# Two token blocks of a pair share one transposition each for h1c and h2c

## The reference

```python
x = x + einsum('bct,bcd->bdt', x, w0[adapter])
x = x + einsum('bsi,io->bso', x, W1) + (x @ A1[adapter]) @ B1[adapter]
x = x + einsum('bsi,oi->bso', x, W2) + 0.5 * (x @ A2[labeler]) @ B2.T
logits = x @ Wr.T + 5.0 * one_hot(language, 8)
gates  = sum over top 2 of one_hot(expert) * softmax(top 2 logits)
x = x + x @ W3.T + 2.0 * einsum('bter,bte,eor->bto', x @ A3, gates, B3)
```

## Time and profile before

| | |
|---|---|
| Median of 3 runs | 521.34 us (521.17 to 521.99) |
| The profiled execution, device time | 521.43 us |
| Its span, first to last instruction | 519.6 us |
| Granted clock of TensorE | 1.00 |
| TensorE, matmul, busy | 515.1 us, 99% |
| DVE busy | 334.2 us, 64% |
| ACT busy | 201.9 us, 39% |
| POOL busy | 170.2 us, 33% |
| Chain that ended last, share on TensorE | 98% |
| Matmuls of `part`, t_hi x em_hi (the costliest line) | 168, 57.3 us, 403 ns each |

### The profile page before, as it was taken

How to read it: one execution, slowest core, us unless ns; L and a number is a source line. 1 busy time by engine, 2 the same in 40 slices (tenths; PEclk the granted TensorE clock), 3 DMA queues, 4 the chain that set the end, 5 groups by cost and what they waited for, 6 DMA issues and landing times.

```text
span 519.6 us, 8870 instructions
## 1 busy us (share of the span) xinstructions
PE 515.1 (99%) x2720; PEld 450.4 (87%) x2720; DVE 334.2 (64%) x655; ACT 201.9 (39%) x351; POOL 170.2 (33%) x250
## 2 busy tenths in 40 slices
PE   8999999999999999999999999999999999999997
PEld 8999999988988888888887888888888888888886
DVE  4798886799533333399876864756647557476464
ACT  5744653345222222267344233323333333233322
POOL 2550000002102020219546544354254434552400
PEclk9999999999999999999999999999999999999999
DMA  7911210214430202040703303313233042222312
GB/s 263 374 65 40 60 40 1 82 40 125 158 112 0 82 0 82 0 166 4 242 2 118 121 23 119 100 47 108 83 117 121 34 117 86 69 87 81 120 32 81
DMA packets 29631, 46.80 MB, mean 90 GB/s; under 512 B 12052, under 2 KB 17940, under 8 KB 29476
## 3 DMA queue, kind: packets, MB, share of 16 engines
q1 hardware_dynamic: 29268, 45.72, 27.3%
q0 software_dynamic: 192, 0.59, 0.3%
q10 hardware_dynamic: 144, 0.13, 0.1%
HBM read 33.39 MB, written 13.04 MB: 89 GB/s over the span
## 4 chain that ended last, share of the span: by engine, by line
PE 98%; DVE 1%; ACT 0%; issue 0%; POOL 0%; POOLq 0%; DVEq 0%; ACTq 0%
PE bank L1893 26%; PE bank L1827 15%; PE bank L1759 11%; PE bank L1882 8%; PE bank L1801 6%; PE bank L1730 5%; PE bank L1813 5%; PE bank L1973 4%; PE bank L1941 4%; PE bank L1949 4%; PE bank L1714 3%; PE bank L1944 1%; PE bank L1943 1%; PE bank L1903 1%; PE bank L1721 1%; PE bank L1930 0%
## 5 line engine op out<-in xcount | busy, mean ns | idle before, releaser
L1893 PE MATMUL bank<-t_hi,em_hi 128*128 128x512 f32 x168 | 57.3, 403 | 0.0
L1183 DVE TENSOR_TENSOR w1t_lo<-raw,w1t_hi 128x1024 fp32r<-128x1024 f32 x18 | 24.1, 1339 | 23.6 <-ACT w1t_hi L909 17.1
L684 POOL TENSOR_TENSOR tmp<-raw 128x512 f32<-128x512 f32 x4 | 7.2, 1793 | 97.2 <-DVE raw L1369 97.2
L1893 PEld LDWEIGHTS bank<-t_hi,em_hi 128*128 128x128 f32 x168 | 31.1, 188 | 7.2 <-DVE em_hi L1183 0.4
L1827 PE MATMUL bank<-te,em_hi 128*128 128x512 f32 x144 | 34.9, 395 | 0.0
L1827 PEld LDWEIGHTS bank<-te,em_hi 128*128 128x128 f32 x144 | 27.0, 188 | 6.6
L670 POOL CAST em_hi<-tba 128x256 fp32r x32 | 13.4, 447 | 58.3 <-PE bank L1882 54.6
L1183 DVE TENSOR_TENSOR em_hi<-tmp,em_hi 128x512 fp32r<-128x512 f32 x22 | 15.1, 688 | 21.7 <-ACT em_hi L1016 12.6
L674 POOL TENSOR_TENSOR em_lo<-tba,em_hi 128x256 fp32r<-128x256 f32 x32 | 27.1, 868 | 2.4 <-POOL em_hi L670 1.2
L1759 PE MATMUL bank<-em_hi,w2s_hi 128*128 128x384 f32 x80 | 27.0, 337 | 0.0
L1759 PE MATMUL bank<-em_lo,w2s_hi 128*128 128x384 f32 x80 | 26.9, 337 | 0.0
(11 more groups left out here) (309 smaller groups left out, 1615.2 us busy)
## 6 DMA issues: line engine op xcount, KB each, us to landing
raw<-in_x_dram SPq DMA_DIRECT2D x16, 512.0 KB, 4.2
b1s<-b1scr SPq DMA_DIRECT2D x32, 217.5 KB, 2.8
raw<-in_b1w_dram SPq DMA_DIRECT2D x10, 512.0 KB, 3.6
out_dram<-ef SPq DMA_DIRECT2D x16, 256.0 KB, 2.1
out_dram<-ost SPq DMA_DIRECT2D x15, 256.0 KB, 2.5
graw<-in_w3a3wr_dram SPq DMA_DIRECT2D x4, 768.0 KB, 11.0
...
```

Source lines behind the costliest of these rows:

```text
L1183: V.tensor_tensor(dst, src, f32(hi), ALU.subtract).then_inc(signal, 1)
L1893: ins = nc.tensor.matmul(to[:, :], left[a][:, k0 + k, :], m_right(right, z, k), start=(name in OPENS and n == 0), stop=(n == 3 * KH - 1), ...
```

## The change

Pair 0, 1 and 7 keep their order. For pairs 2 to 6 (`JOINT`), each engine gets a list of its own:

- h1c of both blocks stand side by side in one tile of 128 columns (without the second copy of the high piece), and TensorE transposes them at once, after three matmuls of p7. The same for h2c, with one transposition after 10 matmuls of p3. Both results lie in bank 6.
- The pieces that are needed more than once are copied by ACT when it empties the bank: four copies instead of one per block for h1T (two for each block), six for h2T (three for each block).
- `h1_into` of both blocks stand after 9 matmuls of p7, `h2_into` of both after 7 of p4. So `route` and `gates` of b0, once beside p6 and p2, and those of b1 come after that. `gated_across` of b0 stands within the `narrow` after p4, that of b1 between tile 1 and tile 2.
- ACT's split of the next pair's XA (`left_hi`) stands ahead of the h2 copies.
- The rows of b1s are interleaved between the two batch rows of a block; in `b1scr` the order of thirds is hi, hi, lo. The place of the bias table goes to h1c; POOL copies the bias elsewhere before pair 0.

The end of the pair's list on DVE, before. gh is the gates' product of b1 (bank 7); em_hi from bank 2 is the split of bank C for tile 2, xb_lo from bank 1 that of bank B for tile 3; the copies to ef and ost3 are tiles 1 and 3; em_lo from bank 5 is `xn_lo`.

The diff, cut to its core:

```diff
-    bias = small("bias", [P, NB, E])
+    bias0 = at("bias0", [P, NB, E], F32, q[0])
+    h1c = small("h1c", [P, 2 * PER * 2 * R1], F32R)
+    assert 2 * PER * 2 * R1 == NB * E
...
+    H1_THREE = h1c[:, 0:2 * SEG1].rearrange("p (t r h) -> p t r h", t=3, h=PER)
+    H1_BOTH = h1c[:, :].rearrange("p (s z r h) -> p s z r h", s=2, z=2, h=PER)
+    H2_BOTH = h2c[:, :, :].rearrange("p (s z) r -> p s z r", s=2)
 
...
+        JOINT = range(2, NP - 1)
+        TH_LAST, HTS_LAST = -2 * len(JOINT), 6 * len(JOINT)
+        SMALL = {n: i + 1 for i, n in enumerate((("mixed", 0), ("mixed", 1), ("h1", 0), ("h1", 1), ("h2", 0), ("h2", 1)))}
+        H1_COPIES, H2_COPIES = 2, 3
+        COPIES = 2 * (H1_COPIES + H2_COPIES)
...
-                    for third, half in enumerate((0, 1, 0)):
+                    for third, half in enumerate((0, 0, 1)):
...
-                    rows = slice(h * SEG1, (h + 1) * SEG1)
+                    rows = slice(h, PER * SEG1, PER)
...
+            pool.wait_ge(s_cst, E + 4)
+            for s in range(2):
+                nc.gpsimd.tensor_copy(BIAS[:, s, :].rearrange("p (b e) -> p b e", e=E), bias0[:, s:NB:2, :]).then_inc(s_bias, 1)
...
+            def h1_both(p):
+                act.wait_ge(s_th, th_joint(p) + 1)
+                for s in range(2):
+                    own = slice(4 * R1 * s, 4 * R1 * (s + 1))
+                    own_hi = slice(4 * R1 * s, 4 * R1 * s + 2 * R1)
+                    nc.scalar.activation(h1T[s][0:4 * R1, :], bank[RT][own, Z1], ACT.Copy).then_inc(s_hts, 1)
+                    nc.scalar.activation(h1T[s][4 * R1:6 * R1, :], bank[RT][own_hi, Z1], ACT.Copy).then_inc(s_hts, 1)
+            def h2_both(p):
+                act.wait_ge(s_th, th_joint(p) + 2)
+                for s in range(2):
+                    own = slice(2 * R2 * s, 2 * R2 * (s + 1))
+                    own_hi = slice(2 * R2 * s, 2 * R2 * s + R2)
+                    nc.scalar.activation(h2T[s][0:R2, :], bank[RT][own_hi, Z2], ACT.Copy).then_inc(s_hts, 1)
+                    nc.scalar.activation(h2T[s][R2:2 * R2, :], bank[RT][own_hi, Z2], ACT.Copy).then_inc(s_hts, 1)
+                    nc.scalar.activation(h2T[s][2 * R2:4 * R2, :], bank[RT][own, Z2], ACT.Copy).then_inc(s_hts, 1)
 
...
+            def joint_pair_hi(p):
+                b0, b1 = 2 * p, 2 * p + 1
+                made = PRODUCTS * p - PRODUCTS
...
+                xn_hi(b1, YB)
+                act.wait_ge(s_sum, 4 * p - 1)
+                operand_hi(XB[0][:, 0:KH, :], tmp[:, :, :])
+                h1_both(p)
+                act.wait_ge(s_wide, made + PRODUCT["p7"])
+                left_hi(p + 1)
+                h2_both(p)
+                xm_hi(0, bank[BA])
+                exp_of(b0)
+                act.wait_ge(s_wide, made + PRODUCT["p3"])
+                xm_hi(1, bank[BD_])
+                ght_hi(b0, 0)
+                exp_of(b1)
+                xn_hi(b0 + 2, YB + 1, 6 * p + SMALL["mixed", 1])
+                act.wait_ge(s_add, 3 * p)
+                act.wait_ge(s_mix, 4 * p + 1)
+                xm_hi(0, bank[BC])
+                ost_even(p, 0)
+                act.wait_ge(s_wide, made + PRODUCT["p4"])
+                act.wait_ge(s_mix, 4 * p + 2)
+                xm_hi(1, bank[BB])
+                ght_hi(b1, 1)
+                ost_even(p, 2)
...
+            def joint_pair_lo(p, steps):
+                b0, b1 = 2 * p, 2 * p + 1
+                ops = OPS * p - OPS
+                operand_lo(CS[1], tmp[:, :, :], CS[0], ops + 2)
+                first_joint(0, 6 * p + SMALL["mixed", 0], steps)
+                operand_lo(DS[1], tmp[:, :, :], DS[0], ops + 3)
+                operand_lo(XB[1][:, :, :], raw[1][:, :, :], XB[0][:, :, :], ops + 4)
+                sum_p1(p)
+                operand_lo(CS[1], raw[1][:, 0:KH, :], CS[0], ops + 5)
+                sum_p5(p)
+                xn_lo(b1, YB)
+                operand_lo(XB[1][:, 0:KH, :], tmp[:, :, :], XB[0][:, 0:KH, :], ops + 6)
+                first_joint(1, 6 * p + SMALL["mixed", 1], steps)
+                second_joint(0, 6 * p + SMALL["h1", 0], steps)
+                sum_p7(p)
+                second_joint(1, 6 * p + SMALL["h1", 1], steps)
+                left_lo(p + 1)
+                route(p, 0, steps, 6 * p + SMALL["h2", 0])
+                xm_lo(0, bank[BA], 4 * p + 1)
+                gates(b0, 0, steps)
+                route(p, 1, steps, 6 * p + SMALL["h2", 1])
+                xm_lo(1, bank[BD_], 4 * p + 2)
+                ght_lo(b0, 0)
+                xn_lo(b0 + 2, YB + 1)
+                gates(b1, 1, steps, b0 + 1)
+                xm_lo(0, bank[BC], 4 * p + 3)
+                xm_lo(1, bank[BB], 4 * p + 4)
+                ght_lo(b1, 1)
+                ost_odd(p, 1)
+                ost_odd(p, 3)
...
-            def narrow(b, left, to):
-
-                pe.wait_ge(s_sel, 4 * b + 4)
-                if isinstance(b, int) and b == 0:
-                    pe.wait_ge(s_s0l, 1)
-                above(pe, s_xnl, b)
-                for k in range(K):
+            def narrow(b, left, to, ks=range(K)):
+                if ks.start == 0:
+                    pe.wait_ge(s_sel, 4 * b + 4)
+                    if isinstance(b, int) and b == 0:
+                        pe.wait_ge(s_s0l, 1)
+                    above(pe, s_xnl, b)
+                for k in ks:
                     for a, z in TERMS:
                         ins = nc.tensor.matmul(bank[to][:, 0:SC], left(a, k), S[z][:, k, :], start=(k == 0 and (a, z) == TERMS[0]),
                                                stop=(k == K - 1 and (a, z) == TERMS[-1]), skip_group_check=True)
-                ins.then_inc(s_nar, 1)
+                if ks.stop == K:
+                    ins.then_inc(s_nar, 1)
 
...
+            def h1_both_across(p):
+                pe.wait_ge(s_h1c, 4 * p + 4)
+                nc.tensor.matmul(bank[RT][:, Z1], f32(h1c[:, :]), ident[:, :], is_transpose=True, start=False, stop=True,
+                                 skip_group_check=True).then_inc(s_th, 1)
+            def h2_both_across(p):
+                pe.wait_ge(s_h2c, 4 * p + 4)
+                nc.tensor.matmul(bank[RT][:, Z2], f32(h2c[:, :, :]).rearrange("p m r -> p (m r)"), ident[:, :], is_transpose=True,
+                                 start=False, stop=True, skip_group_check=True).then_inc(s_th, 1)
...
+            def joint_pair_products(p):
+                b0, b1 = 2 * p, 2 * p + 1
+                ops, sums = OPS * p - OPS, 3 * p - 3
+                h1_there = hts_joint(p) + 2 * H1_COPIES
+                h2_there = hts_joint(p) + COPIES
+                part("p1", 0, 5)
+                mixed(b0, 0)
+                part("p1", 5, 12)
+                pe.wait_ge(s_opl, ops + 2)
+                part("p5", 0, 12)
+                pe.wait_ge(s_opl, ops + 3)
+                part("p6", 0, 12)
+                pe.wait_ge(s_opl, ops + 4)
+                narrow(b1, second_block, YB)
+                pe.wait_ge(s_cp, 2 * p - 1)
+                part("p2", 0, 7)
+                mixed(b1, 1)
+                part("p2", 7, 12)
+                pe.wait_ge(s_add, sums + 2)
+                pe.wait_ge(s_opl, ops + 5)
+                part("p7", 0, 3)
+                h1_both_across(p)
+                part("p7", 3, 9)
+                h1_into_from(h1_there, 0, p)
+                h1_into_from(h1_there, 1, p)
+                part("p7", 9, 12)
+                pe.wait_ge(s_opl, ops + 6)
+                part("p3", 0, 10)
+                h2_both_across(p)
+                part("p3", 10, 12)
+                pe.wait_ge(s_add, sums + 3)
+                part("p4", 0, 7)
+                h2_into_from(h2_there, 0)
+                h2_into_from(h2_there, 1)
+                part("p4", 7, 12)
+                pe.wait_ge(s_opl, ops + 7)
+                narrow(b0 + 2, first_block, YB + 1, range(0, 6))
+                gated_across(b0, 0)
+                narrow(b0 + 2, first_block, YB + 1, range(6, K))
+                tile(p, 0, False, False)
+                tile(p, 1, False, False)
+                gated_across(b1, 1)
+                tile(p, 2, False, False)
+                tile(p, 3, False, False)
```

More of the change, by code:

```diff
@@ L56, in cond_resid_kernel @@
     ROWS = LORA + K
+    NP_ = NB // 2
     F3C = 3 * P
@@ L1520, in first_low_rank, with first_joint, second_joint @@
                     ts, at_ = slice(h * T, (h + 1) * T), C3 + PER * R2 + h * R1
-                    lo(h1c[ts, h * SEG1 + 2 * R1:(h + 1) * SEG1], nar[ts, at_:at_ + R1], h1c[ts, h * SEG1:h * SEG1 + R1], s_h1c)
+                    lo(H1_THREE[ts, 1, :, h], nar[ts, at_:at_ + R1], H1_THREE[ts, 0, :, h], s_h1c)
+            def first_joint(s, there, steps):
+                nar = bank[RT + s]
+                dve.wait_ge(s_small, there)
+                for h in range(PER):
+                    ts, at_ = slice(h * T, (h + 1) * T), C3 + PER * R2 + h * R1
+                    steps.then(V.tensor_copy(H1_BOTH[ts, s, 0, :, h], nar[ts, at_:at_ + R1]))
+                steps.hold()
```

(41 more changed lines are left out.)

56 lines of the change are left out of this document (42 added, 14 removed).

## The result

| | before | after |
|---|---|---|
| Median | 521.39 us (521.17 to 521.99, 5 runs) | 534.08 us (533.72 to 534.69, 5 runs) |
| Ratio after / before, 95% interval | | 1.0242 [1.023, 1.0253] |
| Span of the profiled execution | 519.6 us | 532.2 us |

A forecast was written before the change was run, and what follows sets the result against it. TensorE's chain of slots was taken as the bound; stalls of 0.13 + 0.06 + 0.61 + 0.3 less 0.22 made +0.9 us a joint pair (+0.6 the first), together +4.2, so 525.5 us, range 522.6 to 528.1.

The forecast's parts named there:

- The rest, at nothing: Bias copies, interleaved b1s rows (as many DMAs as before), the split of `narrow` and narrower casts on DVE: no cost.
- Tile 1's copy and SP: Tile 1's copy on DVE ends later, XB follows 11.37 us behind through SP's stores: TensorE stalls about 0.3 us a pair.
- the first has no late XB yet: The first joint pair is spared the XB stall, so it loses 0.6 us instead of 0.9.
- The left operand holds up the h2 copies: Rival, chance 0.08: x lands late, ACT's split delays the six h2 copies, +0.5 us a pair on top, 528.1 us.
- Copies at eviction: ACT's four h1T and six h2T copies fit with 0.13 and 0.4 us spare: no cost.
- Gates of block 0: From the first `h2_into` to gh's end takes 3.48 us against TensorE's 3.39: stall 0.13 us a pair.
- Gates of block 1: On DVE beside POOL's subtractions they take 2.61 us: stalls of 0.06 at gh's transposition and 0.61 at tile 2.
- The rival in which they run clear of it: Rival, chance 0.20: block 1's gates take 1.60 us instead of 2.61, away from POOL; +1.3 in all, 522.6 us.
- Ten transpositions fewer: Two fewer on TensorE in each of five pairs, 0.11 us each: 0.22 a pair, 1.1 us saved.
- Pair 7: Keeps the old order; its spare 0.5 us swallows the 0.3 of late XB; its b1s may come 0.1 late.
- Sums: TensorE slot totals: 3.39 us to block 0's gh, 4.55 from its end to block 1's, 17.8 to XB's use.
- What would show it: Right: TensorE's longest wait at tile 2 (some 0.5), then XB, pairs 0.9 longer; wrong: ACT-copy waits larger than DVE's.

The follow-up runs named there:

- e1: The changed kernel with each batch row's b1s rows in neighbouring partitions again instead of every second one (only the time is read): 527.89 us, ratio 1.0108.
- e9: The changed kernel with one edit: GpSimd's `take` for the second block waits until gh of block 1 is written: 533.62 us, ratio 1.0237.
- e12: The changed kernel with SyncE's loads reordered (pairs 1 to 6), `take` behind the gates, two TensorE steps later, `ght_lo` ahead of bank D's split: 521.07 us, ratio 0.9992.

## Why the prediction was wrong, step by step

- **The rest, at nothing**: the failed step. "b1s rows are interleaved but as many DMAs as before" counted the DMAs and not what each costs SyncE. At 0.51 instead of 0.33 us they add 1.4 us a pair to a chain that the prediction itself had given 0.5 to spare. e1 prices that line at some 6.2 us of 12.7; without it the kernel takes 527.89, inside the forecast range.
- **Tile 1's copy and SP**: right in kind, wrong in size, +1.04 for +0.3. From the copy's end (384.05 + 0.68) to that of XB's low half (395.44 + 1.23) it took 11.94 instead of 11.37, with four of the dear issues in it. The longer gates moved tile 2 and the copy alike: the copy ended 1.34 behind tile 2's first matmul, 1.27 had been forecast. That "the first has no late XB yet" failed too: SyncE's list of pair 1 holds the same issues, TensorE waited 0.6 for XB in the first joint pair, and that pair lost 2.3 instead of 0.6.
- **The left operand holds up the h2 copies**, given 0.08: it came true, with +0.38 a pair. Its condition was a late landing of x; the landing was at least as quick as assumed (3.14), but the issue was not where the earlier trace rows had it. The rival took the issue as fixed behind XB's end, 7.27 us as before; it was 8.11 (396.67 to 404.78). It should have been asked of this rival what else moves the issue, and what follows from tile 1's copy depending on x: a ring, in which a delay is paid in every round instead of once.
- **Copies at eviction**, at nothing: +0.21 at `h1_into`. The copies follow each other at 0.29, not 0.22 (the 0.22 of the earlier trace rows is between instructions of another kind); the prediction had named 0.3 as the point from which 0.1 is lost, and took the lower value.
- **Gates of block 0**: right in kind; 0.29 for 0.13.
- **Gates of block 1**: 2.9 for 2.61 in three of the five pairs, 2.5 in the first and the last; +0.88 for +0.67 in the pair of the table. Right that they stand beside GpSimd's subtractions: with `take` held back they take 1.6 (e9). The rival in which they run clear of it did not occur. The rule of the Trainium skill that was weighed ("SBUF — State Buffer", "Who interferes with whom") agrees in this: the sum gate took 0.38 to 0.66 us beside the subtractions and 0.17 without (e9). But the product gw hardly lost (0.18 against 0.16), and in those three pairs the largest part of the loss stood in gm, a `tensor_scalar` of small tables that the prediction had not named.
- **Ten transpositions fewer**: 0.22 a pair, as e12 shows (34.14 to 33.91). The 81 ns of the Trainium skill ("TensorE: Matmul & The Clock Gate", "Back-to-back issue gap") would have made it an estimated 0.16; the row was right.
- **Pair 7** swallows the 0.3: right, there is no wait for XB in it. But it was 0.6 longer all the same, at its first `h1_into`, where TensorE waited for b1s, which the prediction had 0.1 late: the same issues again.
- **Sums**: 3.39, 4.55 and 17.8 come out only with slots a little over the printed ones (0.233 us for a 512-wide matmul, 0.1115 for a 232-wide one, the means of many starts); with 0.23 and 0.11 they are 3.35, 4.49 and 17.6. No more than 0.2 a pair hangs on it.
- **What would show it**: the longest wait was to be tile 2's, with XB behind. It was XB's, a pair was 2.3 to 2.7 over before instead of 0.9, and the gates of block 1 were about as long as named. Waits on h2T were there, but smaller than those on VectorE, so the sign of an error, as it was written, did not show.
